# An attention and mixture-of-experts block whose attention turns are replanned by 32 places, with three PSUM banks for transposed products

## The reference

```python
mod = (silu(c) @ wmod).reshape(4, 6, 1, -1)
sa, ca, ga, sb, cb, gb = (mod[:, i] for i in range(6))
ga, gb = (sign(g) * maximum(abs(g), 0.25) for g in (ga, gb))
h = layernorm(x) * (1 + ca) + sa
x = x + ga * attention(h, wq, wk, wv, wo)          # softmax(q k^T) v, 16 heads
h = layernorm(x) * (1 + cb) + sb
logits = h @ gate_w.T                               # 32 experts
w = softmax(logits); top 4 of w, scaled to sum 1
out = sigmoid(h @ shared_expert_gate.T) * shared(h) # silu(h Wg) * (h Wu), then down; hidden 512
for e in range(32):
    gate, up = split(h @ gate_up[e].T)
    out = out + w_e[:, None] * ((silu(gate) * up) @ down[e].T)
return x + gb * out
```

## Time and profile before

| what | us |
|---|---|
| median of 3 runs (648.0 to 648.52) | 648.5 |
| the profiled execution: its time | 650.28 |
| the profiled execution: its span, first to last instruction | 648.5 |
| lead, up to the first transposed product | 51.3 |
| turns 0, 1, 2 | 81.5, 81.7, 81.8 |
| turn 3: groups 0 and 1; groups 2 and 3 | 41.2; 28.8 |
| finish | 88.7 |
| routed experts; sum of results | 149.0; 44.5 |

### The profile page before, as it was taken

The page is one execution under the profiler, slowest core; times in us unless marked ns, Lnnn a source line. Parts: engine busy times, 40 slices in busy tenths (PEclk is TensorE's granted clock), DMA queues, the critical chain, the costliest instruction groups (busy, mean ns, idle before and its releaser), DMA issues.

```text
span 648.5 us, 10653 instructions
## 1 busy us (share of the span) xinstructions
PE 584.2 (90%) x3118; PEld 320.4 (49%) x3119; DVE 378.5 (58%) x874; ACT 261.3 (40%) x523; POOL 200.2 (31%) x268
## 2 busy tenths in 40 slices
PE   4999999899998999989999998999889999999271
PEld 3453242234433344332433464565778889889251
DVE  6285757766769667696773665653534444444083
ACT  3214445654666646554456512001234344344100
POOL 6100000000000830007300480362256666666442
PEclk9957999999999999999999999999999999999797
DMA  6142161101401223012100127922455565552393
GB/s 210 37 129 86 34 198 28 30 2 41 83 8 28 90 85 82 6 30 83 50 1 2 41 83 322 266 101 66 121 147 147 156 170 155 163 161 53 107 410 131
DMA packets 41958, 67.17 MB, mean 104 GB/s; under 512 B 9099, under 2 KB 31764, under 8 KB 41564
## 3 DMA queue, kind: packets, MB, share of 16 engines
q1 hardware_dynamic: 29824, 45.62, 24.7%
q0 software_dynamic: 7680, 16.87, 7.5%
q10 hardware_dynamic: 4416, 4.20, 1.9%
HBM read 38.93 MB, written 27.51 MB: 102 GB/s over the span
## 4 chain that ended last, share of the span: by engine, by line
PE 73%; DVE 9%; DMA 5%; issue 4%; ACT 3%; POOL 3%; SPq 1%; POOLq 0%; ACTq 0%; DVEq 0%
PE ps L791 21%; PE ps L804 9%; PE ps L1017 8%; PE ps L1038 6%; PE ps L885 5%; PE ps L743 5%; PE ps L879 4%; DVE max_q L1121 3%; PE ps L1006 3%; PE ps L763 2%; DMA up_sb<-results 2%; PE ps L751 2%; PE ps L817 2%; POOL dispatched L457 2%; ACT probs L625 2%
## 5 line engine op out<-in xcount | busy, mean ns | idle before, releaser
L1121 DVE TENSOR_REDUCE max_q<-ps 128x1 f32<-128x512 f32 x256 | 163.2, 683 | 91.9 <-PE ps L763 90.8
L625 ACT ACTIVATE probs<-ps 128x512 f32<-128x512 f32 x256 | 138.2, 595 | 106.8 <-PE ps L791 106.7
L791 PE MATMUL ps<-q_rows,k_rows 32*128 32x512 f32 x512 | 153.7, 647 | 11.4 <-ACT probs L625 10.3
L763 PE MATMUL ps<-k_rows,q_rows 31*128 31x512 f32 x512 | 155.0, 687 | 0.3 <-DMA k_rows<-qk_raw 0.3
L475 POOL DMA_INDIRECT results<-y_sb,dest x96 | 94.5, 984 | 72.3 <-ACT y_sb L676 37.2
L791 PEld LDWEIGHTS ps<-q_rows,k_rows 32*128 32x128 f32 x512 | 49.0, 185 | 92.6 <-ACT probs L625 56.3
L1017 PE MATMUL ps<-up_sb,oT 128*128 x384 | 70.9, 328 | 1.3 <-issue 1.2
L804 PE MATMUL ps<-probs,v_ext 128*32 128x512 f32 x512 | 68.2, 605 | 0.0
L1017 PEld LDWEIGHTS ps<-up_sb,oT 128*128 128x128 f32 x384 | 61.3, 190 | 2.3 <-issue 2.2
L442 POOL TENSOR_TENSOR rstd<-veps,mhalf 128x4 f32<-128x4 f32 x4 | 4.1, 1037 | 167.4 <-DVE veps L1190 167.3
L763 PEld LDWEIGHTS ps<-k_rows,q_rows 31*128 31x128 f32 x512 | 48.7, 194 | 10.3 <-DVE max_q L1121 6.3
(11 more groups left out here) (172 smaller groups left out, 689.2 us busy)
## 6 DMA issues: line engine op xcount, KB each, us to landing
xe<-dispatched SPq DMA_DIRECT2D x96, 129.0 KB, 2.2
up_sb<-results SPq DMA_DIRECT2D x16, 512.0 KB, 8.5
up_sb<-in_up SPq DMA_DIRECT2D x2, 3072.0 KB, 14.8
dispatched<-pad_rows SPq DMA_DIRECT2D x33, 129.0 KB, 4.8
down_sb<-in_down SPq DMA_DIRECT2D x1, 3072.0 KB, 31.7
x<-in_x ACTq DMA_DIRECT2D x4, 512.0 KB, 5.2
q_rows<-qk_raw SPq DMA_DIRECT2D x64, 32.0 KB, 2.0
k_rows<-qk_raw SPq DMA_DIRECT2D x64, 32.0 KB, 2.0
```

What stands on the lines that cost most here:

```text
L625: act.activation(probs[:, u % 8, :], ps[:, st_bank(t.b, g, u), :], ACT.Exp).then_inc(exp_done, 1)
L763: pe.matmul(ps[:, banks[u % len(banks)], :], q_rows[32 * i:32 * i + ONE, b % 2, g, qt * P:(qt + 1) * P], k_rows[32 * i:32 * i + ONE, b % 2 ...
L791: pe.matmul(ps[:, st_bank(b, g, n), :], k_rows[32 * i:32 * i + 32, b % 2, g, kt * P:(kt + 1) * P], q_rows[32 * i:32 * i + 32, b % 2, g, :] ...
L1121: dve.tensor_reduce(max_q[:, g % 2, qt, i:i + 1], ps[:, banks[(16 * g + n) % len(banks)], :], AXX, ALU.max).then_inc(max_done, 1)
```

## The change

- The plan of a turn is now a table of places (`FIRST` for turn 0, `MIDDLE` for turns 1 and 2, `LAST` for turn 3). Side work of all engines hangs on one number, the place. V0, V1 and QK2 are cut in two halves that stand at two odd places. The two transposes of the batch after next (NT0, NT1) are made at places 30 and 31 instead of TP0 and TP1 in the next turn; turn 0 keeps its own TP0 and TP1 too.
- Bank 7 moves from the side products to the transposed ones: ST = (3, 4, 7), and the wait is on the exponential three units before. All side products of a turn's places share bank 6, but in the second half of the last turn, where they alternate between 7 and 6.
- The four heads' and four tiles' maxima of a group are transposed at once, 16 rows of 128 (one transpose instead of four), so the negated maxima go to the rows by four DMAs instead of one.
- The logits are made with tokens on partitions: 16 matmul passes with 33 columns each from h2T, and LGT and its copy are gone.
- The rows of h2 are modulated by POOL (`scale_and_shift` there, four instructions of 128 x 512), after both transposes. The columns h2T are modulated by ACT's copy out of PSUM, by scale and bias from `modT2`. That is made in turn 0 by a new side product, MODT (16 matmul passes of 4 columns). The finish takes the same course.
- DVE's side work is cut into smaller pieces, at most one or two in a place: `heads_back`, `variances2`, `shifted_logits`, `counts_before`, `slots_out` are new names for parts that stood in larger functions. ACT normalises one tile in a place.
- In the lead, V0 and V1 come after the fourth and eighth score of group 0 instead of before them, and SP places q's rows as soon as q is out, not waiting for k. A new wait holds the third transposed product of turn 0 until V1 of the lead is written out of bank 7.

The diff, cut to its core:

```diff
-    ORDER = (
-        ("MAX0", "att"), ("TP0", "pre"), ("TP1", "pre"), ("QK0", "pre"), ("SG0@0", "fill"),
...
+    FIRST = {"MAX0": 0, "TP0": 1, "TP1": 3, "QK0": 5, "QK1": 7, "MAX1": 8, "MOD0": 9, "MOD1": 11, "V0": (13, 15),
+             "MAX2": 16, "MODT": 17, "QK2": (19, 21), "QK3": 23, "MAX3": 24, "V1": (27, 29), "NT0": 30, "NT1": 31}
+    MIDDLE = {"MAX0": 0, "QK0": 1, "WO0": 3, "WO1": 5, "MAX1": 8, "QK1": 9, "V0": (11, 13), "HT0": 14, "HT1": 15,
+              "MAX2": 16, "LOG": 17, "QK2": (19, 21), "QK3": 23, "MAX3": 24, "RANK": 25, "V1": (27, 29), "NT0": 30, "NT1": 31}
+    LAST = {"MAX0": 0, "SG0@0": 1, "WO0": 3, "WO1": 5, "SU0@0": 7, "MAX1": 8, "SG1@0": 9, "SU1@0": 11, "HT0": 14, "HT1": 15,
+            "MAX2": 16, "LOG": 17, "SG2@0": 19, "SU2@0": 23, "RANK": 25, "SG3@0": 27, "SU3@0": 31}
...
-        SC, ST, O, MISC = (0, 1, 2), (3, 4), 5, (6, 7, 0, 1, 2, 3)
+        SC, ST, O, MISC = (0, 1, 2), (3, 4, 7), 5, (6, 7, 0, 1, 2, 3)
...
-            return ST[n % 2]
+            return ST[(16 * NG * b + 16 * g + n) % 3]
...
-                sp.dma_start(q_rows[ONE:P:P // G, (t.b + (g + 1) // NG) % 2, (g + 1) % NG, :], neg_max[:, :]).then_inc(maxrow, 16)
+                for qt in range(TJ):
+                    sp.dma_start(q_rows[ONE:P:P // G, (t.b + (g + 1) // NG) % 2, (g + 1) % NG, qt * P:(qt + 1) * P],
+                                 neg_max[G * qt:G * qt + G, :]).then_inc(maxrow, 16)
...
+            def scale_and_shift(t):
+
+                p = t.b - 1
+                for k in range(KD):
+                    full(pool, t, f"HT{k}")
...
+                for half in range(2):
+                    two = h2[p % 2][:, 2 * half:2 * half + 2, 0:D]
+                    st.then(pool.tensor_tensor(two, two, mod_b[:, (3 * p + 1) * D:(3 * p + 2) * D].unsqueeze(1).to_broadcast([P, 2, D]), ALU.mult))
+                    st.did(pool.tensor_tensor(two, two, mod_b[:, 3 * p * D:(3 * p + 1) * D].unsqueeze(1).to_broadcast([P, 2, D]), ALU.add))
...
             for t in turns[1:]:
                 deviations2(t)
+                scale_and_shift(t)
                 dispatch(t)
+            scale_and_shift(fin)
             dispatch(fin)
...
-                frees(act.activation(h2T[:, s % (B - 1), k, :], src, ACT.Copy), t, f"HT{k}")
+                if s == 0:
+                    act.wait_ge(modT2_s, 1)
+                frees(act.activation(h2T[:, s % (B - 1), k, :], src, ACT.Identity, scale=modT2[:, bass.ds((2 + k) * B + s, 1)],
+                                     bias=modT2[:, bass.ds(k * B + s, 1)]), t, f"HT{k}")
...
-                for qt in range(TJ):
-                    mm = pe.transpose(bank[0:G, qt * P:(qt + 1) * P], max_q[:, (g + 1) % 2, qt, :], ident[:, :])
-                filled(mm, t, f"MAX{g}")
+                filled(pe.transpose(bank[0:TJ * G, 0:P], max_q[:, (g + 1) % 2, :, :].rearrange("p q i -> p (q i)"), ident[:, :]), t, f"MAX{g}")
...
-                    above(pe, exp_done, 64 * b + u - 1)
+                    if b == 0 and u == 2:
+                        written(pe, lead, "V1")
+                    above(pe, exp_done, 64 * b + u - 2)
...
-                for k in range(KD):
-                    mm = pe.matmul(bank[0:E + 1, :], gate_sb[:, k, :], h2T[:, (t.b - 1) % (B - 1), k, :], start=(k == 0), stop=(k == KD - 1))
+                for j in range(TJ):
+                    for k in range(KD):
+                        mm = pe.matmul(bank[:, 64 * j:64 * j + E + 1], h2T[:, (t.b - 1) % (B - 1), k, j * P:(j + 1) * P], gate_sb[:, k, :],
+                                       start=(k == 0), stop=(k == KD - 1))
...
-                        pe.wait_ge(h2_ready, 2 * t.b)
+                        pe.wait_ge(h2_norm, TJ * t.b)
...
             for n in range(16):
-                score(0, 0, n, SC + ST)
+                score(0, 0, n, SC + ST[0:2])
+                if n in (3, 7):
+                    project_v(lead, n // 4)
...
+                    if place == 18:
+                        top_logits(t)
+                    if place == 19:
+                        top_experts(t)
+                    if place == 20:
+                        shifted_logits(t)
+                    if place == 21:
+                        choices_of_one(t)
+                    if place == 22:
+                        choices(t)
+                    if place == 23:
+                        counts_before(t)
+                    if place == 25:
+                        weights(t)
+                    if place == 26:
+                        ranks_out(t)
+                        slots(t)
+                    if place == 27:
+                        slots_out(t)
+                    if place == 28:
+                        weights_end(t)
```

More of the change, by code:

```diff
@@ L53 @@
 class Turn:
-    ORDER = (
[4 rows of a table removed]
-        ("MAX2", "att"), ("HT0", "post"), ("HT1", "post"), ("LOG", "post"),
-        ("LGT", "post"), ("QK3", "pre"), ("SG2@0", "fill"), ("SU2@0", "fill"),
-        ("MAX3", "pre"), ("SG3@0", "fill"), ("RANK", "post"),
-        ("SU3@0", "fill"))
-    LEAD = tuple((name, "pre") for name in ("TP0", "TP1", "QK0", "QK1", "QK2", "QK3", "V0", "V1", "MAX3"))
+    LEAD = ("TP0", "TP1", "QK0", "QK1", "QK2", "QK3", "V0", "V1", "MAX3")
+    FIRST = {"MAX0": 0, "TP0": 1, "TP1": 3, "QK0": 5, "QK1": 7, "MAX1": 8, "MOD0": 9, "MOD1": 11, "V0": (13, 15),
[4 more added lines that the diff above has]
+            "MAX2": 16, "LOG": 17, "SG2@0": 19, "SU2@0": 23, "RANK": 25, "SG3@0": 27, "SU3@0": 31}
     def __init__(self, b, kinds, used):
@@ L73, in __init__, with at, halves @@
         self.att, self.pre, self.post, self.mod, self.fill = (kind in kinds for kind in ("att", "pre", "post", "mod", "fill"))
-        self.uses = {}
-        for n, name in enumerate(name for name, kind in (self.ORDER if b >= 0 else self.LEAD) if kind in kinds):
-            self.take(name, n % 2, used)
+        self.next = "next" in kinds
+        self.uses, self.places = {}, {}
+        if b < 0:
+            for n, name in enumerate(self.LEAD):
+                self.take(name, n % 2, used)
+        elif self.att:
+            half = 0
+            for name, place in (self.FIRST if self.mod else self.LAST if self.fill else self.MIDDLE).items():
+                if self.next or not name.startswith("NT"):
+                    places = place if isinstance(place, tuple) else (place,)
+                    self.places[name] = places
+                    if self.fill and places[0] >= 16:
+                        half = 1 - half
+                    self.take(name, half, used)
+    def at(self, name, place):
+        return name in self.places and self.places[name][-1] == place
+    def halves(self, name, place):
+        places = self.places.get(name, ())
+        if place not in places:
+            return ()
+        return (0, 1) if len(places) == 1 else (places.index(place),)
     def take(self, name, m, used):
@@ L88 @@
 class Finish(Turn):
-    CHAIN = {1: ("WO0", "WO1"), 6: ("HT0", "HT1"), 7: ("LOG",), 8: ("LGT",),
-             12: ("RANK", "CNT"), 16: ("TAB",)}
+    CHAIN = {1: ("WO0", "WO1"), 6: ("HT0", "HT1"), 7: ("LOG",), 11: ("RANK", "CNT"), 15: ("TAB",)}
     def __init__(self, b, used):
@@ L942, in turn @@
                                     score(t.b + 1, g - 2, n)
[L943 to L944 removed]
+                        for n in range(u, u + step, 2):
+                            between(t, 8 * g + n // 2)
             def finish(t):
```

401 lines of the change are left out of this document (210 added, 191 removed), and 3 rows, old and new, of the table ORDER.

## The result

The changed kernel takes 623.26 us (median of 4 runs, 622.21 to 624.79), the kernel before beside it 648.25 (645.54 to 648.52). The ratio is 0.9613, with a 95% interval of 0.9584 to 0.9642. The forecast was 622.0 with a range of 612 to 636. The profiled execution took 622.21 us, with a span of 620.5.

The account below looks back on a forecast made before the run. PE's own work was taken to bound dense places, ACT's exponential loop thin ones. Turns (-6.2, -6.8, -7.4, -3.3), finish -1.5, lead -1.9 and POOL +0.6 gave -26.5: 622.0 us, range 612 to 636.

Parts of the forecast that it names:

- The bound: Turns: PE's own work bounds places dense with side work; the loop through ACT's exponential bounds thin ones, 1.81 us a round.
- The rival that the bank gives nothing: Turns: untransposed products hold up the quad as before, so only removed work counts; 640 us, chance 6%.
- Turns 1 and 2: Turn 1 falls from 81.7 to 74.9 us (-6.8), turn 2 from 81.8 to 74.4 (-7.4).
- Waits of DVE: Places 21, 22 and 26 to 28: DVE side work over 0.77 us stalls PE, about 1.8 us in turns 1 and 2 each.
- Turn 0: Falls from 81.5 to 75.3 us (-6.2), with 2.0 for the cold start and 1.8 for modulation chains at places 9 and 11.
- Lead, turn 3: Lead -1.9 us by sending q's rows early and moving V0, V1; turn 3 -1.6 in groups 0, 1 and -1.7 in 2, 3.
- ScalarE and GpSimd: Turns: POOL's four instructions, 1.5 us each, and ACT's added work stay hidden; +0.6 us in all for POOL.
- The contention: POOL and DVE hold each other up in SBUF, 0 to 1.5 us a turn, taken as 0.2; DVE's place 17 product at risk.
- The finish: After the turns: HT's 1.19 us wait for DVE and LGT's 0.4 go; -1.5 us, between 0 and -4.
- The sum: Whole kernel: turns, finish, lead and POOL add to -26.5 us, from the 648.5 median to 622.0.
- DVE's pace in the second halves: Second halves of turns: DVE takes 2.5 us a place instead of 2.1, stalling PE 4 us more a turn; 633, chance 18%.
- The slower case: One bank for all side products holds PE some 0.7 us at each of some 68 products; 670 us, chance 4%.

Follow-up runs that it names:

- the fastest: Changed kernel with untransposed banks counted through batches and, in the finish, DVE's counts and weights two products later, GpSimd's rows early: 615.80 us.

## Why the prediction was right

**The bound.** That PE lost time to ACT in thin places, and in dense ones only its own work counted, is borne out in kind: the row of waits for ACT went from 10.3 us to 0.2. The row is no measure of the gain, though: the bank alone had nearly the same waits gone (0.8 us are left of them in its profile) and no gain. And dense places had paid a little too: a pair with a whole product took 5.28 us before and takes 5.06 with three banks. The rival that the bank gives nothing (640) is refuted for this plan, where the bank carries 9.0 to 9.9 us, and true in number for the old one, where it carries 0.5. Its mechanism, quads held by the untransposed products, is not what that kernel shows: the bank gained 2.6 us in its turn 2, and the shared side bank took 2.3 of them back. The working had treated the parts as a sum. They aren't one.

**Turns 1 and 2.** Forecast 74.9 and 74.4, measured 74.5 and 73.9. The terms: a whole product at an odd place 1.91 (places of 2.98), a half 1.06 (forecast 1.05; places of 2.13), LOG 1.90 (1.9), the turning 0.20 (0.21), an empty odd place 1.97 (1.9). Waits of DVE were put at 1.8 a turn in places 21, 22 and 26 to 28. There they came to 0.3. The total of waits is still 1.65, because place 16 gave 1.0 and place 0 gave 0.3, which the working did not have. That step was right in its sum by luck and wrong in its places: I had read the wait for the maxima as "three before" everywhere, and at the passage to the next batch the bank of product 63 is handed to product 0, which has to wait for all 64.

**Turn 0.** Forecast -6.2, measured -5.4. `modulation` cost 0.9 in place 11 and nothing in place 9, not 1.8. Place 16 has 0.5 us of the same wait as in turns 1 and 2. The start at the lower clock was longer in some executions than in others: turn 0 took 77.2 us in the changed kernel and 80.0 in the one with GpSimd after the choice, and their code is the same there. Of the 2.8 us between them 1.3 lie in places 1 and 2, and 1.5 in places 18 to 20, where the clock fell once more (0.53 from 97.40 to 100.70). So some 1.4 us of the -5.4 are luck, and with the clock of the kernel before the turn would have gained about 4.0.

**Lead, turn 3.** -2.3, -1.7 and -1.4, for -1.9, -1.6 and -1.7. The first maximum was forecast near 26.4 and starts at 25.92.

**ScalarE and GpSimd.** Forecast +0.6. GpSimd's instruction takes 1.18 us, not the 1.5 that I scaled from the earlier trace rows, and hides in the turns. The contention was put beside DVE's product of place 17. Its one visible effect on PE was through a cast in the finish, where the wait of PE is 3.51 us, about 1.0 of it from this (2.52 with the rows on DVE).

**The finish.** Forecast -1.5, measured -3.2. HT's wait of 1.19 is gone, LOG takes 1.71 and LGT is gone. But the kernel before had a stretch at lower clock there, right behind PE's wait of 2.40 us for DVE, and the changed one had none:

```profile
402.00:411.20 9.20, 8.88 (x35) 7.62 (x36) 3.92 (x14) 0.00 (x0) 0.00 (x0) 0.81 1.09 370
```

At full clock that stretch would be 1.7 us shorter (9.20 x 0.19). Without it the finish differs by -1.5. The forecast is met only with this correction, and the finish of the kernel with the banks counted through, which had such a stretch too, gives the same: 86.48 against 88.01. So does the old finish without one, in the kernel with the bank alone: 86.32 against the changed kernel's 84.77.

**The sum.** Forecast -26.5, measured -25.0 by the medians. The cost of a place and the floor of an empty one were sized right; that stages with errors of their own (the forecast of turn 0 too good, the waits for DVE in other places, GpSimd's cost in the finish) add up so well is in part luck.

**The rivals.** DVE's pace in the second halves (+4 a turn) did not come: in the second half of turn 1 DVE is busy for 1.0 to 2.0 us in the even places of 2.07, and place 26 alone, at 2.32 with DVE busy for 2.18, is longer for it. With the rows on DVE one more place gives way. The slower case, one side bank at 0.7 us a product, is refuted by the time itself and by the kernel with two side banks, which is no faster than its like with one. Its mechanism is real, at 1.06 to 1.24 us, where two side products stand with no quad between them; the new plan has no such spot in the turns, and the prediction had not named that as the point from which it decides.

## What to carry to other kernels

Moving a buffer from one user to another can gain in one place and lose as much in another: here it brought 0.5 us alone and 9 to 10 once the plan kept the users of the shared bank apart. Look at buffer and plan together, and at every spot where two users of a shared bank follow each other directly. Where a helper engine is given long instructions, place them beside steps of the other engine that they do not shut out. A ring of buffers that is counted anew in each round deserves a look of its own: where the number of uses is no multiple of the ring, the first use of a round can fall on the buffer of the last. Cut long side work to the size of the gap that the loop leaves, and count the empty places that this fills.

## What the runs showed of the hardware

- GpSimd's 1.18 us on 128 x 512 held up DVE steps of 0.17 us until its end, three in a row (0.51, 1.01, 0.89), and others between them not at all.
- The clock at the start of turn 0 differed between executions. The first row is of the changed kernel's first 6 us; the next 6 us had full clock there. Over the same two windows it was 0.50 and 0.99 in the kernel before, and 0.50 and 0.70 in the one with the rows on DVE.

```profile
49.05:55.05 6.00, 6.00 (x29) 2.64 (x29) 2.58 (x4) 2.98 (x6) 0.00 (x0) 0.70 0.14 50
```

- Between this start and the routed experts' first 25 us the clock came down again in single stretches of some 3.3 us at 0.50 (one of 6.3), one to three in a profile, those of 3.3 worth some 1.7 us each. Most come after PE has waited or run narrow products. In the finish ten of the eleven kernels have PE waiting for 2.4 to 4.4 us, and seven of them then have a mean clock of 0.70 or less over the next 5.6 us (the kernel before, both with two transposed banks, the rows on DVE, the banks counted through, GpSimd after the choice, the routing chain cut); three do not (the changed kernel, the bank alone, the whole products), though the changed kernel's wait is 3.51 us and one of 2.38 was enough elsewhere. The eleventh, the fastest, has no wait over 0.81 us inside the finish and no such stretch. In turn 0 five of the nine kernels with the new plan have one in places 18 and 19, in four of them right behind MODT, 16 passes of four columns; the changed kernel is not among the five. Here it is in the kernel with the routing chain cut, whose last pass of MODT begins at 94.1:

```profile
94.30:97.60 3.30, 3.30 (x17) 0.67 (x16) 1.59 (x5) 1.26 (x3) 0.00 (x0) 0.51 1.08 251
```

What decides between the executions stays open.

- The last stretch, whose code no kernel changes, took 190.0 to 193.7 us in the eleven profiled executions. The first 25 us of it had a clock of 0.93 in some, one such stretch, and 1.00 in others, which does not account for all of it: the fastest kernel has 0.93 there and 190.73 us in all, the changed one 0.93 and 193.58. What makes the rest of the difference stays open. It is why single profiles are compared here by stage, and kernels by their medians.
